# Attention head pipeline: the steps of the softmax division on other slots, ten DMA issues per head merged, rows of maxima earlier in SyncE's order

## The reference

```python
c = einsum('bhsd,hld->bhsl', xh, Wdkv); c = layernorm(c) * ln_g + ln_b
q_lat = einsum('bhsd,hdl->bhsl', xh, einsum('hij,hlj->hil', Wq, Wuk))
scores = einsum('bhsl,bhtl->bhst', q_lat, c) / sqrt(L)      # causal mask, then
w = softmax(scores)
v = einsum('bhsl,hld->bhsd', c, Wuv)
oh = einsum('bhst,bhtd->bhsd', w, v)                        # then Wo_h, Wo, bo
x + attention(xn) + mean over top 2 of relu(xn @ expert_w[e] + expert_b[e])
```

## Time and profile before

| | |
|---|---|
| runs | 1737.16, 1737.25, 1741.39 us; median 1737.25 |
| profiled execution | 1736.69 us, span 1734.9 us |
| mean granted PE clock | 0.969 |
| busy, share of the span | PE 88%, DVE 67%, ACT 52%, POOL 33% |
| DMA issues from SP per head | 7 loads, 1 expert weight, 16 rows of maxima, 16 sums and denominators, 1 + 1 + 4 + 4 for the division |

### The profile page before, as it was taken

How to read it: one execution, slowest core, us unless ns; L and a number is a source line. 1 busy time by engine, 2 the same in 40 slices (tenths; PEclk the granted TensorE clock), 3 DMA queues, 4 the chain that set the end, 5 groups by cost and what they waited for, 6 DMA issues and landing times.

```text
span 1734.9 us, 45239 instructions
## 1 busy us (share of the span) xinstructions
PE 1531.7 (88%) x12544; PEld 845.8 (49%) x12545; DVE 1157.8 (67%) x2501; ACT 896.8 (52%) x1628; POOL 579.6 (33%) x780
## 2 busy tenths in 40 slices
PE   4788859899899999999999999999999959999996
PEld 2677845444444444444444444444445425555443
DVE  4777777677777777777777777777777614444467
ACT  1656635565656656665656566665666623333200
POOL 1333312776222222223222222222222333333276
PEclk8999978999999999999999999999999979999998
DMA  5467760232222222232223222232223145555499
GB/s 163 150 207 239 216 177 17 61 91 63 63 62 74 78 64 63 59 90 65 61 61 84 68 65 62 66 87 62 64 59 93 41 157 177 174 171 174 135 362 344
DMA packets 165707, 198.15 MB, mean 114 GB/s; under 512 B 50144, under 2 KB 99296, under 8 KB 165248
## 3 DMA queue, kind: packets, MB, share of 16 engines
q1 hardware_dynamic: 146880, 157.10, 30.8%
q0 software_dynamic: 12992, 35.77, 6.8%
q10 hardware_dynamic: 5760, 4.49, 0.8%
HBM read 108.99 MB, written 62.98 MB: 99 GB/s over the span
## 4 chain that ended last, share of the span: by engine, by line
PE 39%; SPq 25%; issue 11%; DVE 9%; DMA 7%; POOL 4%; ACT 3%; ACTq 0%; DVEq 0%; POOLq 0%
PE PS L1205 12%; PE PS L1258 12%; PE PS L1301 11%; SPq L428 7%; SPq L421 4%; POOL w_hi L688 4%; SPq L443 3%; DVE pm L1017 3%; SPq L441 3%; SPq L440 3%; DMA arena<-mxT 3%; DMA arena<-in_x 2%; PE PS L1283 2%; DVE bv_bc L1038 1%; ACT arena L787 1%
## 5 line engine op out<-in xcount | busy, mean ns | idle before, releaser
L1017 DVE TENSOR_REDUCE pm<-PS 128x1 f32<-128x512 f32 (+3 forms) x1280 | 716.0, 602 | 243.8 <-PE PS L1205 238.1
L1205 PE MATMUL PS<-arena 97*64 97x512 f16 (+7 forms) x5120 | 732.0, 354 | 110.0 <-DVE pm L1017 39.2
L787 ACT ACTIVATE arena<-PS 128x512 f32<-128x512 f32 (+1 forms) x1152 | 603.7, 574 | 356.1 <-PE PS L1205 355.0
L1258 PE MATMUL PS<-arena 128*33 128x512 f32 (+3 forms) x2560 | 655.4, 532 | 0.0
L1205 PEld LDWEIGHTS PS<-arena 96*64 96x64 f16 (+1 forms) x5120 | 355.8, 110 | 490.9 <-issue 189.2
L605 POOL TENSOR_SCALAR_AFFINE_SELECT arena<-arena 128x256 f32<-128x256 f32 (+1 forms) x256 | 110.8, 433 | 637.2 <-ACT arena L787 636.3
L1258 PEld LDWEIGHTS PS<-arena 128*33 128x33 f32 x2560 | 169.5, 111 | 82.5 <-issue 0.7
L1301 PE MATMUL PS<-w_hi,arena 128*128 x576 | 172.7, 382 | 0.8 <-issue 0.8
L1205 PE MATMUL PS<-later,deny 128*64 128x128 f16 x1024 | 166.2, 222 | 0.0
L804 ACT ACTIVATE arena<-PS 128x1024 f16<-128x1024 f32 x72 | 73.7, 1024 | 152.4 <-PE PS L1283 152.4
L1068 DVE SCALAR_TENSOR_TENSOR arena<-PS,eb_bc 128x512 f32<-128x512 f32 x72 | 49.8, 691 | 130.3 <-PE PS L1301 127.9
(11 more groups left out here) (172 smaller groups left out, 1311.9 us busy)
## 6 DMA issues: line engine op xcount, KB each, us to landing
expert_rows<-arena SPq DMA_DIRECT2D x72, 256.0 KB, 2.1
comb_hl<-arena SPq DMA_DIRECT2D x256, 64.0 KB
arena<-q_pieces SPq DMA_DIRECT2D x96, 128.0 KB
arena<-k_pieces SPq DMA_DIRECT2D x96, 128.0 KB
v_rows<-arena SPq DMA_DIRECT2D x8, 1056.0 KB, 6.6
arena<-v_rows SPq DMA_DIRECT2D x32, 264.0 KB
arena<-in_x SPq DMA_DIRECT2D x8, 1024.0 KB, 7.3
xn_rows<-arena SPq DMA_DIRECT2D x16, 512.0 KB, 6.1
```

Source lines behind the costliest of these rows:

```text
L787: a.activation(probs[kk % 4][:, a_ * CH:a_ * CH + w], PS[:, s2_bank(k, x), 0:w], ACT.Exp, scale=SCALE).then_inc(s["exp_done"], 1)
L1017: v.reduce_max(pm[:, c, r, p:p + 1], PS[:, S1_BANK[n], 0:w], AX).then_inc(s["s1_done"], 1)
L1205: last = t.matmul(PS[h:h + P // 2, bank, cols], lhsT[:, h:h + P // 2], rhs, start=start, stop=stop)
L1258: last = t.matmul(PS[rows_, 6 + c % 2, CH - wds[a]:CH], v_sb[pu % 2][:, j + a, :], probs[pk % 4][:, a * off:a * off + wds[a]], start=p_ in ...
```

## The change

- ROW_LAG goes from 2 to 1, and in SP's `heads` the rows of maxima are issued ahead of everything else in their slot. They stand in slots 0, 8, 10 and 14 then.
- ADD goes from slot 5 to 6, HI from 14 to 15, LO from 15 to 16, KEEP from 16 to 18; the loop's boundary goes with KEEP from slot 18 to 20.
- The sums of a head are laid out with chunk c in every fourth row (4d + c in place of 32c + d), both halves in one tile `pair`. With that the inverses come back in one DMA, the results are kept in one, and the two denominators of a chunk go out in one: 4 x 1 + 3 + 3 = 10 fewer DMAs per head. The counts of the semaphores follow.

```diff
--- before.py
+++ after.py
@@ -166,7 +166,7 @@
         mx16 = sb("mx16", [P, NC, TR], f16)
         mxT = sb("mxT", [P, NC, TR], f16)
         rest = comb_hl[:, :, :, :].rearrange("p a k e -> p (a k e)")
-        sums_a, sums_b = ([rest.bitcast(f32)[:, (2 * half + w) * CH:(2 * half + w + 1) * CH] for w in range(2)] for half in range(2))
+        pair = [rest.bitcast(f32)[:, 2 * w * CH:2 * (w + 1) * CH].rearrange("p (a q) -> p a q", a=2) for w in range(2)]
         inv = bv_bc[:, 0:CH]
         o_st = sb("o_st", [P, 2, CH], f16)
         den = sb("den", [P, 2, S // P], f32)
@@ -308,13 +308,13 @@
         NP_ = len(PIECES)
 
 
-        PV_LAG, ROW_LAG = 2, 2
+        PV_LAG, ROW_LAG = 2, 1
         S1_FROM = 8
 
-        MOVE_LAG, DEN_LAG, ADD_LAG, REC_LAG, INV_LAG, BACK_LAG = (PV_LAG + d for d in (1, 3, 4, 6, 7, 9))
-        MUL_LAG, HI_LAG, LO_LAG, KEEP_LAG = (PV_LAG + d for d in (12, 13, 14, 15))
+        MOVE_LAG, DEN_LAG, ADD_LAG, REC_LAG, INV_LAG, BACK_LAG = (PV_LAG + d for d in (1, 3, 5, 6, 7, 9))
+        MUL_LAG, HI_LAG, LO_LAG, KEEP_LAG = (PV_LAG + d for d in (12, 14, 15, 17))
         HEAD_END = NU - 1
-        OT_OUT = 16 * 4 * NC // 2
+        OT_OUT = 16 * 3 * NC // 2
         SPLIT = (13, 14, 15)
         LEAD = range(KEEP_LAG + 1)
         SPAN = range(KEEP_LAG + 1, 2 * NU + KEEP_LAG + 1)
@@ -436,17 +436,20 @@
                 if c == 0:
                     sp.wait_ge(s["mul_done"], count(hd - 1))
                 sp.sem_inc(s["move_at"], 1)
-                r = slice(HD * c, HD * (c + 1))
-                sp.dma_start(sums_a[u][r, :], o[0:HD, :]).then_inc(s[f"ot_out{c % 2}"], 16)
-                sp.dma_start(sums_b[u][r, :], o[2 * HD:3 * HD, :]).then_inc(s[f"ot_out{c % 2}"], 16)
                 for a in range(2):
-                    sp.dma_start(den_dram[ds(hd, 1), a, c * CH:(c + 1) * CH],
-                                 o[2 * HD * a + HD:2 * HD * a + V1, :]).then_inc(s[f"ot_out{c % 2}"], 16)
+                    sp.dma_start(pair[u][c:P:NC, a], o[2 * HD * a:2 * HD * a + HD, :]).then_inc(s[f"ot_out{c % 2}"], 16)
+                sp.dma_start(den_dram[ds(hd, 1), :, c * CH:(c + 1) * CH].rearrange("o a q -> (o a) q"), o[HD:2 * HD + V1:2 * HD, :]
+                             ).then_inc(s[f"ot_out{c % 2}"], 16)
 
             def heads(j, more, span):
                 for kk in span:
                     w, k = divmod(kk, NU)
                     hd, u = j * HPB + w, w % 2
+                    hk = kk - ROW_LAG
+                    if 0 <= hk and (hk < HPB * NU or more):
+                        for ahead, n in slot_pieces(hk % NU):
+                            if n in CHUNK_END and (hk // NU + ahead < HPB or more):
+                                max_row(j * HPB + hk // NU + ahead, (hk // NU + ahead) % 2, CHUNK_END[n])
                     if k == MOVE_LAG and w > 0 and (w < HPB - 1 or more):
                         sp.wait_ge(s["pv_done"], count(hd * NU))
                         sp.sem_inc(s["move_at"], 1)
@@ -458,11 +461,6 @@
                     hk = kk - MOVE_LAG
                     if 0 <= hk and (hk < HPB * NU or more) and hk % NU in LAST:
                         ot_moves(j * HPB + hk // NU, hk // NU % 2, LAST[hk % NU])
-                    hk = kk - ROW_LAG
-                    if 0 <= hk and (hk < HPB * NU or more):
-                        for ahead, n in slot_pieces(hk % NU):
-                            if n in CHUNK_END and (hk // NU + ahead < HPB or more):
-                                max_row(j * HPB + hk // NU + ahead, (hk // NU + ahead) % 2, CHUNK_END[n])
                     hk = kk - DEN_LAG
                     if 0 <= hk and hk % NU == HEAD_END:
                         hd = j * HPB + hk // NU
@@ -485,17 +483,15 @@
                         sp.sem_inc(s["move_at"], 1)
                         sp.wait_ge(s["o_lo_done"], count(hd))
                         sp.sem_inc(s["move_at"], 1)
-                        for c in range(NC):
-                            sp.dma_start(inv[HD * c:HD * (c + 1), :],
-                                         inv_dram[ds(hd, 1), c * CH:(c + 1) * CH].to_broadcast([HD, CH])).then_inc(s["inv_in"], 16)
+                        sp.dma_start(inv, inv_dram[ds(hd, 1)].to_broadcast([HD, S])
+                                     ).then_inc(s["inv_in"], 16)
                     hk = kk - KEEP_LAG
                     if 0 <= hk and hk % NU == HEAD_END:
                         w, hd = hk // NU, j * HPB + hk // NU
                         sp.wait_ge(s["o_lo_done"], count(hd + 1))
                         sp.sem_inc(s["move_at"], 1)
-                        for c in range(NC):
-                            sp.dma_start(attnT[HD * w:HD * (w + 1), ds(j, 1), c].rearrange("p o z q -> p (o z) q"),
-                                         o_st[HD * c:HD * (c + 1)]).then_inc(s["o_out"], 16)
+                        sp.dma_start(attnT[HD * w:HD * (w + 1), ds(j, 1)].rearrange("p o c z q -> p (o c z q)"),
+                                     o_st[:, :, :].rearrange("p z q -> p (z q)")).then_inc(s["o_out"], 16)
 
             load_head(0, 0)
             load_head(1, 1)
@@ -516,7 +512,7 @@
                 sp.dma_start(out_v[q % B][ds(m * (OUT_RING // B) + q // B, 1)].rearrange("t p d -> (t p) d"), acc[q]
                              ).then_inc(s[f"out_done{q}"], 16)
 
-            sp.wait_ge(s["o_out"], count(16 * NC * BH))
+            sp.wait_ge(s["o_out"], count(16 * BH))
             sp.dma_start(rest, comb_dram).then_inc(s["comb_in"], 16)
             for q in range(OUT_RING):
                 residual(0, q)
@@ -610,7 +606,7 @@
                 for par in range(2):
                     pool.wait_ge(s[f"ot_out{par}"], count((hd + 1) * OT_OUT))
                 pool.sem_inc(s["sum_at"], 1)
-                g.tensor_tensor(sums_a[u], sums_a[u], sums_b[u], ALU.add).then_inc(s["sum_done"], 1)
+                g.tensor_tensor(pair[u][:, 0], pair[u][:, 0], pair[u][:, 1], ALU.add).then_inc(s["sum_done"], 1)
 
             def low_part(hd):
 
@@ -777,7 +773,7 @@
                     if 0 <= hk and hk % NU == HEAD_END:
                         hd = it * 2 + hk // NU
                         act.wait_ge(s["mul_done"], count(hd + 1))
-                        act.wait_ge(s["o_out"], count(hd * (16 * NC)))
+                        act.wait_ge(s["o_out"], count(hd * 16))
                         a.activation(o_st[:, 0], inv, ACT.Copy).then_inc(s["o_hi_done"], 1)
                     if kk < 2 * NU or more:
                         k = kk % NU
@@ -790,7 +786,7 @@
                     if 0 <= pk and (pk < 2 * NU or more) and pk % NU in LAST:
                         q = (pk // NU) * NC + LAST[pk % NU]
                         act.wait_ge(s["pv_done"], count(it * (2 * NU) + pk + 1))
-                        act.wait_ge(s[f"ot_out{q % 2}"], count((it * NC + q // 2) * (16 * 4)))
+                        act.wait_ge(s[f"ot_out{q % 2}"], count((it * NC + q // 2) * (16 * 3)))
                         a.activation(ot[q % 2][0:2 * HD + V1, :], PS[0:2 * HD + V1, 6 + q % 2, :], ACT.Copy).then_inc(s["ot_done"], 1)
 
             heads(0, True, LEAD)
@@ -1033,9 +1029,9 @@
 
             def scale(hd, u):
 
-                dve.wait_ge(s["inv_in"], count((hd + 1) * (16 * NC)))
+                dve.wait_ge(s["inv_in"], count((hd + 1) * 16))
                 dve.wait_ge(s["sum_done"], count(hd + 1))
-                v.tensor_tensor(inv, inv, sums_a[u], ALU.mult).then_inc(s["mul_done"], 1)
+                v.tensor_tensor(inv, inv, pair[u][:, 0], ALU.mult).then_inc(s["mul_done"], 1)
 
             def heads(it, more, span):
                 for kk in span:
@@ -1312,7 +1308,7 @@
             pe.wait_ge(s["gT_done"], count(PT))
             pe.wait_ge(s["half_done"], count(PT))
 
-            pe.wait_ge(s["o_out"], count(16 * NC * BH))
+            pe.wait_ge(s["o_out"], count(16 * BH))
             pe.wait_ge(s["comb_in"], count(16))
             def project(m, q, again):
                 u, at = q % B, q // B * P
```

## The result

The changed kernel takes 1765.22 us (median of 4, 1761.71 to 1769.38) against 1738.75 us for the kernel before beside it: a ratio of 1.0161 with a 95% interval of 1.0135 to 1.0186. It is slower by 1.6%, where 1691 us and a range of 1678 to 1724 were forecast.

The account below looks back on a forecast made before the run. PE was taken to set the pace in attention, leaving only its stops to gain, with SP's in-order queue holding the path. Terms 32.6 + 10 + 7.5 + 1.5 - 6 = 45.6 us off gave about 1691 us, range 1678 to 1724.

Parts of the forecast that it names:

- Row 3 in time: Slot 12 of a head: the maxima of query chunk 3, issued earlier by SP, arrive before PE wants them; 32.6 us off.
- The way back of the inverses: SP's later read back in one 256 KB transfer lands after 2.1 us; DVE waits 0.2 us a head, 6 us on.
- (a): Rival: inverses land 2.6 us after issue, the skill page's time; DVE waits 0.7 us a head, 1706 us; chance 0.15.
- Rival (b): Late inverses make DVE wait 1.3 us a head and PE with it; 1724 us; chance 0.18 together with another rival.
- (c): Rival: a wait on the inverses of about 1.7 us a head returns the whole gain; 1737 us; chance 0.08.
- rival (d): The single read back with repeated source is slow, landing after 5.7 us; PE stands in slot 13; 1799 us; chance 0.09.
- Denominators: On SP, one transfer replaces two, four times a head; loads go out 0.42 us earlier, 10 us off PE's waits.
- Strided sums at today's price: On SP, issuing a transfer of the sums to every fourth partition still takes today's 0.54 us.
- Steps set apart: ACT copies the high part a slot later, so exponentials no longer queue behind its wait for DVE's product; 7.5 us off.
- Tail: After the last head, fewer transfers shorten the uncovered chain; 1.5 us off, between 3 off and 3 on.

## Why the prediction was wrong

The sum had the right mechanism at the right place, with three terms mis-sized and one missing.

- **Row 3 in time, 32.6 us: right.** Row 3 left 12.49 us behind row 2's start, forecast 12.45, and PE's wait for it is gone.
- **The way back of the inverses, "6 us on": the step that failed, together with the clock below.** The start was forecast well (893.6, that is 20.7 behind row 2; measured 20.9). PE and with it DVE were some 0.5 us further ahead than counted (ready at 22.05, forecast 22.55). The landing was the large miss. The text took 2.1 us from a 256 KB store in the expert stage; one transfer with a repeated source lands after 3.1 us, near the 3.2 us that stood there as the upper bound. The wait is 2.07 us in the head shown and 1.7 on average (51.6 us over 30 heads), not 0.2. A wait of over 1 us was the prediction's own first sign of being wrong. The fit from the Trainium skill's page "DMA: Bandwidth & Descriptors", section on the anatomy of one DMA, which is for DMAs that GpSimd issues, gives an estimate of 2.6 us and is also too low for this transfer. (The prediction calls the page's case "the second rival below"; it is (a), the first.)
- **The clock: missing.** The prediction read "full granted clock" from slices whose 9 means 0.9 or more, took it as a given, and priced a stop of PE by its length alone. Rival (b) named this stop, in this place, at 1.3 us a head, and gave 1724; (c) gave no net gain for 1.7 us. Now 28 stops are 1.8 us or longer, the matmuls behind 19 of them run at half clock, and PE is 19.3 us longer busy. The missing clock of 33 us is enough for that; that the whole 19.3 us comes from it fits the run with the stop made by hand, but is not shown by itself. By the waits alone the change costs 10.7 us. The trace before did hold the warning: its one slice in the attention with less than the full clock, shown above, is also the one with two stops of 2.0 and 2.1 us (timeline of PE of the kernel before):

```profile
322.24 0.84 PE L1205 MATMUL PS<-arena 97*64 97x512 f16 x6 [2.01 <-DMA arena<-mxT]
...
329.71 0.41 PE L1205 MATMUL PS<-arena 96*64 96x512 f16 x2 [2.13 <-DVE pm L1017]
```

- **Slower: rival (d) had the sign, not the size.** It decided from a landing of 3.6 us and worked with 5.7. Because of the clock and of PE being further ahead, 3.1 us was enough. Four transfers in place of the one are slower still (1.047), so the single transfer is not the fault.
- **Denominators, "10 us off": mis-sized.** A pair took 0.69 us; the merged one takes 0.60 (854.99), not 0.27, so it saves 0.09 us. The loads' wait went from 15.0 to 14.2 us only. On the other chip the changed kernel has 11.0. Where the rows stayed in their old place it did fall, to 5.4 and 6.6 us. Why it falls there and less here stays open.
- **Strided sums at today's price: right.** Two of them take 1.16 us (0.58 each, before 0.54 to 0.59). To strided rows from DRAM an issue does cost more, 0.65 against 0.47, which the change avoids by having one.
- **Steps set apart, 7.5 us off: right in kind.** PE's wait for ACT went from 7.5 to 2.6 us.
- **Tail, 1.5 us off: nothing in the end.** The wait for the first gather went from 18.6 to 18.0 us; the single read back took 2.8 us there. But from the last matmul of the attention to the end it is 340.7 us, against 340.1 before, which lies within the 3 us either way that the prediction allowed.

## What to carry to other kernels

When a queue is reordered to bring one item forward, price what is pushed back against the moment at which its reader will be there, and that reader comes earlier by all that the change saves; here the item pushed back lost more than the one brought forward won, and putting one DMA ahead of another that nobody was waiting for turned +1.1% into -3.1% (each against the kernel before on its own chip). Count a stop of TensorE by its length only while it stays about as short as those that the trace already holds at full clock. For a transfer of a kind that the trace does not have, compute the forecast at both bounds before trusting its middle.

## What the runs showed of the hardware

- Behind a stop of PE of 1.8 us or more came some 3 us or more at half clock with PE busy in 19 of 28 cases in the changed kernel, in 25 of 26 with the order alone, and in 16 of 25 equal stops of 2.42 us made by hand; behind 27 stops of 1.24 us (the run with one extra instruction) it never came. What decides between stops of the same length stays open. The Trainium skill's page "TensorE: Matmul & The Clock Gate", part 1, on the HAM clock gate, states two levels, 2.4 and 1.2 GHz, and this case's 0.50 of 2.4 GHz agrees with its lower one.
- One DMA of 256 KB from DRAM with each row read 32 times lands 2.8 to 3.2 us after issue, 3.1 at the median; four of 64 KB to strided rows are complete 4.2 us after the first issue.
- A DMA of two rows of 2 KB from SBUF to DRAM holds SP for 0.60 us, where one row took 0.27.
